# A two-layer graph network on one core: splitting every attention tile, with whole-tile casts and the bias added by DMA

## What is computed

```
# layer 0, an attention layer with the softmax over axis 1
h  = x @ W0;  f1 = h @ a1;  f2 = h @ a2
e  = f1 + f2^T;  e = where(e >= 0, e, 0.2 * e)
att = softmax(adj * e, axis=1)
x' = att @ h + bias + x
# layer 1, a convolution with batch normalization over all nodes of all graphs
s  = x' @ W1 + b1;  y = adj @ s
out = relu((y - mean) * rsqrt(var + eps) * gamma + beta) + x'
```

## Time and profile before

| | before |
|---|---|
| median of three runs | 984.5 us |
| profiled execution: time / span | 981.78 us / 980.0 us |
| granted TensorE clock | 0.986 |
| TensorE matmul busy | 914.9 us (93%), 3055 |
| VectorE busy | 696.0 us (71%), 864 |
| ScalarE busy | 802.3 us (82%), 953 |
| GpSimd busy | 439.8 us (45%), 334 |
| DMA | 213.91 MB, mean 218 GB/s |

### The profile page before, as it was taken

The page is one execution under the profiler, slowest core; times in us unless marked ns, Lnnn a source line. Parts: engine busy times, 40 slices in busy tenths (PEclk is TensorE's granted clock), DMA queues, the critical chain, the costliest instruction groups (busy, mean ns, idle before and its releaser), DMA issues.

```text
span 980.0 us, 9394 instructions
## 1 busy us (share of the span) xinstructions
PE 914.9 (93%) x3055; PEld 528.9 (54%) x3055; DVE 696.0 (71%) x864; ACT 802.3 (82%) x953; POOL 439.8 (45%) x334
## 2 busy tenths in 40 slices
PE   7998999989999899999999899998999999998970
PEld 4333555555555655556555555556555555555760
DVE  2544477777777867777777967778777777779967
ACT  6877599986999789996999779996999969896746
POOL 1544355562555435562555635553555625554000
PEclk9999999999999999999999999999999999999995
DMA  8956454566456664566456664475546555435968
GB/s 321 422 227 223 158 197 169 215 227 215 176 183 233 212 220 167 214 221 225 172 183 225 225 219 156 168 265 202 204 182 225 190 218 204 168 128 193 385 253 342
DMA packets 45132, 213.91 MB, mean 218 GB/s; under 512 B 5406, under 2 KB 6030, under 8 KB 23438
## 3 DMA queue, kind: packets, MB, share of 16 engines
q1 hardware_dynamic: 45084, 213.32, 59.7%
HBM read 189.07 MB, written 24.23 MB: 218 GB/s over the span
## 4 chain that ended last, share of the span: by engine, by line
PE 79%; DVE 6%; issue 6%; POOL 4%; ACT 3%; DMA 0%; DVEq 0%; SPq 0%; ACTq 0%; POOLq 0%
PE acc L441 40%; PE acc L406 11%; PE acc L421 6%; PE acc L422 6%; PE acc L420 6%; POOL hz L793 3%; PE acc L428 3%; DVE exp_lo L675 3%; PE acc L390 2%; DVE stats L695 2%; PE acc L455 1%; PE acc L457 1%; PE acc L458 1%; ACT scores L542 1%; DVE adj_slot L781 1%
## 5 line engine op out<-in xcount | busy, mean ns | idle before, releaser
L656 DVE CUSTOM_DVE_ANT_0 scores<-scores,adj_slot 128x2048 f32<-128x2048 f32 x128 | 294.0, 2297 | 24.0 <-DMA adj_slot<-adjT 21.4
L675 DVE TENSOR_TENSOR exp_lo<-scores,exp_hi 128x512 fp32r<-128x512 f32 x336 | 268.5, 849 | 35.5 <-ACT exp_hi L552 35.4
L542 ACT ACTIVATE scores<-scores,neg_mx 128x2048 f32<-128x2048 f32 x128 | 256.3, 2002 | 4.2
L793 POOL TENSOR_TENSOR hz<-region_even,rz 128x128 f32<-128x128 f32 x64 | 132.6, 2072 | 222.1 <-DVE rz L663 222.1
L441 PE MATMUL acc<-adj_slot,region_even 128*128 128x512 f32 x512 | 228.8, 592 | 0.0
L552 ACT CAST exp_hi<-scores 128x512 fp32r<-128x512 f32 x336 | 190.6, 615 | 41.0 <-PE acc L422 37.5
L793 POOL TENSOR_TENSOR hz<-region_odd,rz 128x128 f32<-128x128 f32 x64 | 124.2, 1940 | 215.4 <-DVE rz L663 215.4
L420 PE MATMUL acc<-exp_hi,hz_lo 128*128 128x512 f32 x336 | 162.1, 482 | 15.6 <-DVE exp_lo L675 8.7
L441 PE MATMUL acc<-adj_slot,region_odd 128*128 128x512 f32 x392 | 175.2, 592 | 0.0
L406 PE MATMUL acc<-scores,hz 128*128 128x512 f32 x352 | 158.7, 595 | 6.2 <-POOL hz L793 5.0
L441 PEld LDWEIGHTS acc<-adj_slot,region_even 128*128 128x128 f32 x512 | 96.7, 190 | 106.2 <-issue 103.4
(11 more groups left out here) (75 smaller groups left out, 676.5 us busy)
## 6 DMA issues: line engine op xcount, KB each, us to landing
adj_slot<-adjT SPq DMA_DIRECT2D x128, 1024.0 KB, 4.8
adj_slot<-xT SPq DMA_DIRECT2D x13, 1024.0 KB, 9.6
adj_slot<-xp_dram SPq DMA_DIRECT2D x8, 1024.0 KB, 6.3
adj_slot<-y_dram SPq DMA_DIRECT2D x7, 1024.0 KB, 6.6
outT<-adj_slot SPq DMA_DIRECT2D x6, 1024.0 KB, 4.7
f_odd<-f_rows SPq DMA_DIRECT2D x4, 1024.0 KB, 6.9
region_even<-xT SPq DMA_DIRECT2D x16, 256.0 KB, 5.5
f_even<-biasT SPq DMA_DIRECT2D x16, 256.0 KB, 6.8
```

What stands on the lines that cost most here:

```text
L542: act.activation(scores[e][:, :], scores[e][:, :], ACT.Exp, bias=neg_mx[:, e:e + 1], accum_out=zsum[:, e:e + 1]).then_inc(exp_done, 1)
L656: dve.tensor_tensor_reduce(scores[e][:, :], scores[e][:, :], slots[s][:, :], 1.0, NEG_BIG, ALU.mult, ALU.max, mx[:, e:e + 1]).then_inc(max ...
L675: dve.tensor_tensor(exp_lo[e][:, cols(c)], scores[e][:, cols(c)], exp_hi[c][:, :].bitcast(F32), ALU.subtract).then_inc(lo_done, 1)
L793: scaled = pool.tensor_tensor(hz[e][:, :], region[bt.par][:, tile_cols(t)], rz[:, e:e + 1].to_broadcast([P, P]), ALU.mult)
```

## The change

- All 16 tiles of batches 1 to 7 are split, not 12. The cast of a tile is one instruction of 2048 columns into one of two new buffers (`hi`, HR = 2), and so is the subtraction; only tile 15 still goes in four pieces. `exp_high` of tile t waits for TensorE's tile t-2.
- TensorE runs the first pass (`hz_lo` with `hi`) over all four chunks, then the second, then the third, and waits for the low part only before the third.
- `f1_all` is one buffer. Its next load waits for the last `edge` of the batch.
- The bias is no longer loaded and added on GpSimd: GpSimd issues a DMA that adds `biasT` onto `region` in place. There are four in a batch.
- x for `make_h` is loaded into `region` of the next parity (`load_x_for_h`), after y has been stored from it and its statistics taken; for batch 1 it lies in a `hi` buffer. Adjacency tile 1 of the next batch is loaded right behind that. `SIGMA` becomes 2 to 15, then 0, 1. SyncE issues the last residual load behind the stores of y.
- The negated maximum moves from ScalarE to VectorE, and so does `y_from_psum`.
- The order on ScalarE becomes exp(t), exp_high(t), edge(t+2); at the end of a batch edge 0, edge 1, exp 0 and exp_high 0 of the next batch precede `h_from_psum`. On VectorE score(t+1) precedes recip(t) and exp_low(t); in the last step y is copied and its statistics are taken before exp_low(15); then score of the next tile 0, `make_xp`, recip and exp_low of the next tile 0, and only then `support_from_psum`.

```diff
-    SPLIT = [t for t in range(NT) if t % 4]
+    HR = 2
+    PARTS = {t: (NC if t == NT - 1 else 1) for t in range(NT)}
...
-    SIGMA = list(range(PRE, NT - 2)) + [1, NT - 2, NT - 1, 0]
+    SIGMA = list(range(PRE, NT)) + list(range(PRE))
...
+            def load_x_for_h(bt, c):
+                sp.wait_ge(y_stored[c], 16 * (bt.n - 1))
+                sp.wait_ge(stats_done, NC * (bt.n - 2) + c + 1)
+                sp.dma_start(region[bt.par][:, cols(c)], xT[bt.n][:, cols(c)]).then_inc(xh_loaded[c], 16)
...
             def load_f1(bt):
+                sp.wait_ge(edge_out, NT * bt.n)
+                sp.dma_start(f1_all[:, :], f_rows[bt.n - 1].partition_broadcast(P)).then_inc(f1_loaded, 16)
...
-                        if k == 14:
-                            load_bias(bt)
-                    load_residual(bt, 3)
+                        if k == 14 and not is_last(bt):
+                            load_f1(nx)
                     for c in range(NC):
                         sp.wait_ge(y_out, NC * pv.n + c + 1)
                         sp.dma_start(y_dram[pv.n][:, cols(c)], region[pv.par][:, cols(c)]).then_inc(y_stored[c], 16)
+                    load_residual(bt, 3)
+                    if not is_last(bt):
+                        for c in range(NC):
+                            load_x_for_h(nx, c)
+                        load_adj(nx, 1)
                 store_xp(bt)
-                if not is_last(bt):
-                    sp.wait_ge(h_mm, NC * (nx.n + 1))
-                    load_adj(nx, 1)
...
             def layer0_split(bt, t):
-                for c in range(NC):
-                    pe.wait_ge(lo_done, chunk_count(bt.prev(), t, c))
-                    pe.matmul(acc0[c][:, :], hz_lo[e][:, :], exp_hi[c][:, :], start=False, stop=False)
-                    pe.matmul(acc0[c][:, :], hz_hi[m % 2][:, :], exp_hi[c][:, :], start=False, stop=False)
-                    pe.matmul(acc0[c][:, :], hz_hi[m % 2][:, :], exp_lo[e][:, cols(c)], start=False,
-                              stop=(t == NT - 1)).then_inc(split_used, 1)
+                for i in range(PARTS[t]):
+                    pe.wait_ge(hi_done, part_count(bt, t, i))
+                    for c in part_chunks(t, i):
+                        wait_acc0(bt, t, c)
+                        pe.matmul(acc0[c][:, :], hz_lo[e][:, :], hi[m][:, cols(c)], start=(t == 0), stop=False)
+                for c in range(NC):
+                    pe.matmul(acc0[c][:, :], hz_hi[m][:, :], hi[m][:, cols(c)], start=False, stop=False)
+                for i in range(PARTS[t]):
+                    pe.wait_ge(lo_done, part_count(bt, t, i))
+                    for c in part_chunks(t, i):
+                        l0_done(pe.matmul(acc0[c][:, :], hz_hi[m][:, :], exp_lo[e][:, cols(c)], start=False,
+                                          stop=(t == NT - 1)), t, c)
...
             def exp(bt, t):
-                act.wait_ge(max_done, NT * bt.n + t + 1)
-                act.mul(neg_mx[:, e:e + 1], mx[:, e:e + 1], -1.0).then_inc(neg_done, 1)
...
             def step(bt):
-                if not is_first(bt):
-                    y_from_psum(bt.prev())
                 if not is_last(bt):
+                    edge(nx, 0)
                     edge(nx, 1)
+                    exp(nx, 0)
+                    exp_high(nx, 0)
                     h_from_psum(nx, acc1)
...
+                    if t == NT - 1 and not is_first(bt):
+                        y_from_psum(bt.prev())
+                        y_stats(bt.prev())
+                    if t > 0 and not is_first(bt):
+                        exp_low(bt, t)
                 if not is_last(bt):
                     score(nx, 0)
...
                 for c in range(NC):
-                    support_from_psum(bt, c)
+                    make_xp(bt, c)
                 if not is_last(bt):
                     recip(nx, 0)
+                    exp_low(nx, 0)
+                for c in range(NC):
+                    support_from_psum(bt, c)
...
             def add_bias(bt, c):
                 pool.wait_ge(x_loaded[c], 16 * (bt.n + 1))
-                pool.wait_ge(bias_loaded[c], 16 * (bt.n + 1))
-                pool.tensor_tensor(region[bt.par][:, cols(c)], region[bt.par][:, cols(c)],
-                                   f1_all[bt.par][:, cols(c)], ALU.add).then_inc(xb_done, 1)
+                pool.dma_start(region[bt.par][:, cols(c)], biasT[:, cols(c)], accum_op=ALU.add).then_inc(xb_done[c], 16)
```

More of the change, by code:

```diff
@@ L64, in build @@
     ER = 4
-    SPLIT = [t for t in range(NT) if t % 4]
+    HR = 2
+    PARTS = {t: (NC if t == NT - 1 else 1) for t in range(NT)}
+    NL = sum(PARTS.values())
     LAST_SPLIT = list(range(1, NT))
-    WHOLE = [t for t in range(NT) if t not in SPLIT]
-    NS = NC * len(SPLIT)
-    SIGMA = list(range(PRE, NT - 2)) + [1, NT - 2, NT - 1, 0]
-    assert NT % ER == 0 and len(SPLIT) % 2 == 0 and NT - 1 in SPLIT and 0 in WHOLE
+    SIGMA = list(range(PRE, NT)) + list(range(PRE))
+    assert NT % ER == 0 and NT % HR == 0
     assert F == P and B == 8 and NT == 16 and sorted(SIGMA) == list(range(NT))
@@ L78, in slot_of @@
         return NT + t if (par and t < PRE) else t
-    X_STAGE = {0: slot_of(1, 0), 1: slot_of(1, 1), **{b: NT - B + b for b in range(2, B)}}
-    STAGED = set(X_STAGE[b] for b in range(1, B))
+    X_STAGE = {b: NT - B + b for b in range(2, B)}
+    STAGED = set(X_STAGE.values())
     F_STEP = {b: (3 * b - 2) // 2 for b in range(1, B)}
@@ L130, in build @@
         bn = sb("bn", [P, 4])
+        x0_sb, x1_sb = slots[NT], hi_x[0]
+        sup_hi = hi[0]
         wt_sb = scores[ER - 1][:, 0:P]
@@ L175, in build @@
         hz_scaled = sem("hz_scaled")
-        ident_set, hz_done, xb_done = sem("ident_set"), sem("hz_done"), sem("xb_done")
+        ident_set, hz_done = sem("ident_set"), sem("hz_done")
+        xb_done = [sem(f"xb_done{c}") for c in range(NC)]
         def cols(c):
@@ L241, in build @@
             earlier[s] += 1
-        for b in range(2, B):
-            earlier[slot_of(b % 2, 1)] += 1
         pieces = [(b, cols(c)) for b in (B - 1, 0) for c in range(NC)] + [(b, slice(0, N)) for b in range(1, B - 1)]
@@ L509, in _ @@
                 pe.wait_ge(f1_out, c + 1)
-                make_h(Batch(0, 0, 0), slots[X_STAGE[0]], acc0, c)
+                make_h(Batch(0, 0, 0), x0_sb, acc0, c)
             pe.wait_ge(w1_loaded, 16)
@@ L524, in edge @@
                 if t == 0 and not is_first(bt):
-                    act.wait_ge(f1_loaded[bt.par], 16 * (bt.half + bt.par))
+                    act.wait_ge(f1_loaded, 16 * bt.n)
                 if t == 0 and is_first(bt):
@@ L545, in exp_high @@
             def exp_high(bt, t):
-                e, m = t % ER, SPLIT.index(t)
+                e, m = t % ER, t % HR
                 act.wait_ge(exp_done, NT * bt.n + t + 1)
-                for c in range(NC):
-                    act.wait_ge(split_used, NS * bt.n + NC * (m - 1) + c + 1)
-                    act.copy(exp_hi[c][:, :], scores[e][:, cols(c)]).then_inc(hi_done, 1)
+                if t >= HR:
+                    wait_l0(act, bt, t - HR)
+                elif bt.n == 1:
+                    act.wait_ge(h_mm, NC * 2)
+                else:
+                    wait_l0(act, bt.prev(), t - HR + NT)
+                for i in range(PARTS[t]):
+                    act.copy(hi[m][:, part_cols(t, i)], scores[e][:, part_cols(t, i)]).then_inc(hi_done, 1)
             def adj_high(bt, m):
@@ L713, in step @@
                 for t in range(NT):
-                    if t > 0 or is_first(bt):
-                        score(bt, t)
-                    if t - 1 in SPLIT and not is_first(bt):
-                        exp_low(bt, t - 1)
-                    if t > 0 or is_first(bt):
+                    if t + 1 < NT:
+                        score(bt, t + 1)
+                    if is_first(bt) or t > 0:
                         recip(bt, t)
@@ L722, in step @@
                         f_from_psum()
-                if not is_first(bt):
-                    exp_low(bt, NT - 1)
-                if not is_first(bt):
-                    y_stats(bt.prev())
-                for c in range(NC):
-                    make_xp(bt, c)
+                    if t == NT - 1 and not is_first(bt):
+                        y_from_psum(bt.prev())
+                        y_stats(bt.prev())
+                    if t > 0 and not is_first(bt):
+                        exp_low(bt, t)
                 if not is_last(bt):
@@ L756, in _ @@
             dve.wait_ge(b1_loaded, 16)
+            score(Batch(0, 0, 0), 0)
             steps(dve, step)
@@ L816, in step @@
                     scale_h(bt, t)
-                    if t == NT - 2 and not is_first(bt):
-                        add_bias(bt, 0)
-                        add_bias(bt, 1)
-                for c in range(0 if is_first(bt) else 2, NC):
+                    if t % TC == TC - 1 and t > TC and not is_first(bt):
+                        add_bias(bt, t // TC - 1)
```

(1 more changed line is left out.)

168 lines of the change are left out of this document (79 added, 89 removed).

## The result

The changed kernel takes 997.6 us (995.7 to 1001.7), the kernel before, run beside it, 983.6: ratio 1.015, interval 1.011 to 1.019. It is slower by 1.5%; forecast were 947 and faster. The profiled execution took 1001.7, its span is 999.9.

What follows compares the result with a forecast made beforehand. TensorE, busy 93% of the span, was taken as the bound. Terms -19.9 - 12.0 - 3 - 3.7 = -38.6 from 981.8 give 943.2, 945.9 referred to the median, plus 1: 947 us, range 938 to 967.

Steps and rivals of the forecast that it cites:

- Part 1: Mid-batch, batches 1 to 7: four more split tiles in each save 19.9 us; the new matmul order costs nothing.
- Part 2: Mid-batch: ScalarE's loop takes 5.88 us a tile, under TensorE's 6.16 by 0.28, so TensorE stays the bound.
- rival A: Mid-batch: ScalarE becomes the bound at 6.4 us a tile; 971 us at most, 958 if half; chance 0.12.
- rival B: GpSimd's three scalings a tile may each wait 2.50 us; 957 us if only at the ends; chance 0.12.
- Part 3: Batch ends: layer 1 starts at E + 15.2, not E + 17.2 (E: tile 13's end); six ends give -12.0 us.
- upper bound of 9.9: Batch end: longest time allowed for the accumulating bias DMA, range 3.8 to 9.9 us, 6.8 taken.
- Rival C: Bias DMA holds the batch ends: 972 us, still faster (chance 0.12), or 997 with a 13 us DMA (chance 0.05).
- Part 4: Batch 0: ends at 98.5 to 99.5 instead of 106.86, but its handover gets worse; net -3 us (0 to -4).
- Part 5: Last batch's end: support's chunk 0 at E + 12.4, where layer 1 started at E + 16.1; -3.7 us.

Runs made afterwards that it cites:

- run 4: Changed kernel with the three passes of a tile chunk by chunk again, as in the kernel before; 1003.0 us, ratio 1.022.
- run 3: Changed kernel with the reciprocal of tile 1 before the score of tile 2 in batches 1 to 7; 976.7 us, ratio 0.994.
- run 5: Changed kernel without bias DMAs, without the second load of x, and with reciprocal 1 before score 2; 952.3 us, ratio 0.970.
- run 6: Changed kernel with reciprocal 1 before score 2 and without bias DMAs; 957.4 us, ratio 0.975.
- run 12: Changed kernel, reciprocal 1 first, bias summed in DRAM a batch ahead: x copied at k = 5, sums at t = 8, 10, 12, 14; 963.0 us, ratio 0.978.
- run 1: Changed kernel without the bias DMAs, so the bias isn't added; 975.9 us, ratio 0.992.
- run 2: Changed kernel without the second load of x, so make_h multiplies what lies in the region; 977.9 us, ratio 0.995.
- run 7: Changed kernel with the bias added to x in DRAM mid-batch, a batch ahead, by four accumulating DMAs in a row; 1023.8 us, ratio 1.043.
- run 9: Changed kernel with bias summed in DRAM by four DMAs in a row, x through the adjacency slot, and reciprocal 1 first; 999.0 us, ratio 1.018.
- run 10: Changed kernel, reciprocal 1 first, bias summed in DRAM a batch ahead: x copied at k = 1, sums at t = 4, 7, 10, 13; 992.0 us, ratio 1.010.

## Why the prediction was wrong

**Part 1** held: every tile of batches 1 to 7 is split, 6.17 apart in mid-batch. That the order costs nothing held too; run 4 shows that it gains some 5 us, at tile 15.

**Part 2** held for ScalarE, against rival A: the casts wait for TensorE, not the other way round. It failed in one clause, "mid-batch I take TensorE as the bound and cost the rest at nothing". The loop was checked in its steady state only, not for the first two tiles after an end, when VectorE has the backlog. That is 26.1 us, and run 3 takes back 20.9. It is rival B in mechanism: its three scalings of 2.50 do come in a row, but once a batch. It was priced at +10 ("1.5 x 7"), and with the clock behind it was 3.7 a batch. The Trainium skill (SBUF — State Buffer, "Who interferes with whom") states that a VectorE instruction with two inputs in SBUF contends with a GpSimd instruction that reads SBUF. Scores and low parts are such instructions, and the rows agree: 0.40 alone, 2.37 to 2.46 beside them. The prediction drew on that section only for descriptors.

**Part 3** failed, and it is the step named as the weakest. The engines' side was right: without a late DMA `make_h` starts at E + 5.95 (5.9), and an end takes 14.99 in runs 5, 6 and 12 (15.2). Two DMA terms were mis-sized, each taken by itself from one row of the kernel before. The load of x, by 3.45 of the earlier trace rows "wanted at 6.0 but harmless until 7.9", let `make_h` start at 8.4 to 10.9; it waited 2.2 to 5.0 us in the six ends. It was issued in time, at E + 1.7, and took 6.6 to 9.3 us until `make_h` could start. The page of the kernel before had a warning, a median well above 3.45 for loads of this kind:
```profile
region_even<-xT SPq DMA_DIRECT2D x16, 256.0 KB, 5.5
```
The bias DMA, "I take the 6.8 of the plain bias load ... landing at 11.6", was issued at 5.9 (4.8) and took 9 us to `make_xp`, at 15.1; over the six ends it was issued at 5.8 to 7.4 and took 7.7 to 10.2. The upper bound of 9.9 held the duration in five of six, but the sum did not ask what the change itself moves into this stretch: 1 MB of x per end and the accumulating DMA, on engines whose share was 0.84 or more in every window shown. (The kernel as a whole moves 213.91 MB before and after.) The prediction also leaves out the store of x', 7.0 in this stretch; in the four ends whose chain shows it, it landed 0.05 to 1.1 us ahead of the support. Nor does it have the granted clock: with the new waits TensorE ran some 3 to 6 us mostly at 0.50, where the waits of 1.02 and 1.30 (run 6) are followed by groups at their usual 0.89. In the third and the fourth end that makes eight groups 10.0 and 9.7 us long instead of 7.1, and only by this does the way over x end last there. By the Trainium skill (DMA: Bandwidth & Descriptors, "Anatomy of one DMA") an estimate for the bias DMA is 2.6 us; the trace does not agree: 4.0 at least, 7.1 in the median, 10.1 at most.

**Rival C** had the mechanism of the slower outcome: `make_xp` 3 waiting for the bias DMA, the reciprocal behind it. It put the price at 3.2 an end and the turning point at 11.5 us of DMA, since it held all else at the forecast. The DMA never took that long. C and B came together, with a loss of 25.6 and 26.1, each under its own turning point, and none of the rivals was a sum of two. C's time of 997 lies beside the measured 997.6 by chance: it stands for a DMA of 13 us, and the longest took 10.1.

**Part 4** was 5.5 too low: layer 0 of batch 0 ended at 103.8, not 99, and layer 1 of batch 1 began at 116.5, not 111. TensorE's timeline has no gap from 22.8 to 103.8, at a granted clock of 1.00 from 25 us on: it does 16 tiles and seven groups of f rows there, at 3.45 to 3.63 each, 81.1 in all, where the prediction counted 22 at 3.43, 75.5. Cast 0 waited for `make_h` as forecast. This was read from the trace, and no run tried it. **Part 5**: 13.9 instead of 12.4, and here the bias DMA was in time (the last `make_xp` at E + 10.3). TensorE's `make_support` of the last batch, first in the changed kernel, then in run 1:
```profile
919.11 5.47 PE L443 MATMUL acc<-w_sb,region_odd 128*128 128x128 f32 x32 [2.30 <-DVE region_odd L711]
```
```profile
893.71 3.84 PE L443 MATMUL acc<-w_sb,region_odd 128*128 128x128 f32 x32 [2.30 <-DVE region_odd L711]
```
The wait is the same 2.30, but the granted clock of the 3 us behind it is 0.57 in the first and 1.00 in the second, and the 32 matmuls take 2.0 us longer from start to next start (5.67 and 3.67). Run 1's end takes 12.1; runs 5 and 6, also without bias DMA, have the low clock there and take 13.7 and 13.5. The prediction priced these matmuls at full clock. In the changed kernel the support also waits 2.19 us for the store of x', until 924.04, and that way ends 0.2 us after the matmuls; so the clock alone would not have given these 2.0 us back.

What stays open: why the granted clock falls behind one wait and not behind another of the same length; why the two DMAs take as long as they do, since a full queue is read from the windows and from runs 1, 2 and 5, and no run changed the traffic alone; and why the fourth issue in a row waits.

## What to carry to other kernels

A change that moves transfers into a stretch must be costed against the sum of all that the DMA engines carry there, not with each transfer's median: look at the DMA share by windows first, and take a price from a stretch as full as the new one. Check a loop's slack also for the first tiles after a stall, in the order in which each engine issues: an instruction that is ready but stands behind one that waits for a DMA (here a reciprocal of 0.16 us) can cost 20 us. An addition moved from an engine to an accumulating DMA is cheap only where nobody waits for it; moved a batch ahead, spaced and away from the adjacency loads, and with the reciprocal first, it made the same change 2.2% faster than the kernel before.

## What the runs showed of the hardware that I had not expected

- GpSimd's fourth DMA issue in a row waited: 3.7 us in batch 0 of the changed kernel, 9.1 to 12.8 in run 7 and 8.4 to 12.5 in run 9, after three of 0.84 to 0.89. Spaced by 9 to 20 us (runs 10 and 12) none waited.
- An accumulating DMA of 256 KB took 7.1 us in the median (4.0 to 10.1) from issue to landing into SBUF, and 5.3 into DRAM (run 12).
- Behind TensorE's six waits for x of 2.2 to 5.0 us in the changed kernel the granted clock was 0.50 for 3 to 6 us; behind the waits of 1.8 to 2.1 for `hz_lo` in four of seven places. Behind waits for x of 2.29 and 2.37 in run 1, and behind five of six waits of 1.62 in run 5, it stayed at 1.00. So the length of a wait does not tell by itself whether the clock falls; where it did, the wait cost up to about twice its length.
- The same 0.40-us scaling on GpSimd takes 2.4 us when VectorE's instructions follow each other without a gap, and ends within 0.3 us of the end of the one that it started beside.
